# A graph network kernel on one core: the last large loop in another order, and its residual added by an accumulating transfer

## The chip, the cores and the metric

The kernel runs on one NeuronCore of a Trainium2 chip. The metric is the device time of one execution in microseconds (us), less is better. The engines are named as the profile names them: PE (TensorE) multiplies matrices, DVE (VectorE) works element by element and reduces, ACT (ScalarE) applies functions and copies, POOL (GpSimd) issues the transfers that need software, and SP (SyncE) issues the plain ones. Each engine runs its own list of instructions in order and waits on semaphores.

## The reference, cut to what matters

Four layers of a graph network run over 10,000 rows of 512 numbers, with 2,500 edges between them. After each layer the row is added to the layer's output and normalised. In float32 throughout:

```
x1 = LN(x + L0(x))                         # messages over the edges, then two dense products on all rows
p  = mean of neighbours @ W_l + b_l + x1 @ W_r
x2 = LN(x1 + leaky(batchnorm(p)) + x1)     # L1 adds its own input once more: 2 * x1 + leaky(...)
x3 = LN(x2 + L2(x2))                       # L2 and L3 are not zero only on rows that are the source of an edge
out = LN(x3 + L3(x3))                      # attention over the edges
```

`leaky(v)` is `max(v, 0.01 v)`, and the batch norm is one scale and one shift for each column. A row that is no source of an edge gets nothing from L2 and L3. For it the output is three layer norms in a row of `2 * x1 + leaky(scale * p + shift)`, which are folded into one with a changed epsilon. The kernel calls these the plain rows and computes them for all rows; the rows with edges are overwritten at the end.

## The kernel before

Rows are padded to 10,240, which makes 80 tiles of 128. The edges make 20 tiles of 128 (`EDGE_TILES`). Phases follow one another: messages, dense products over all tiles, aggregation, edge rows, then `values_phase`, which this change edits, and `attended_rows_phase`, which overwrites the rows with edges. Tables such as `p`, `x1`, `sum2` and `state` lie in memory (HBM).

`values_phase` is one software pipeline, unrolled in Python over `STEPS` = 25 steps. In step `s` tile `a = s` has its sums turned and multiplied, tile `b = s - 1` goes through the second product and a layer norm, tile `c = s - 2` gets queries and keys, tile `d = s - 3` scores, tile maxima and weighted values, and tile `e = s - 4` is merged into `state`. What a tile needs from another engine is reached by semaphores that count tiles.

For the maximum of a tile (`tile_maximum`, from L1762) the 8 scores of each of the 128 edges go to memory (`aw_rows`, issued by SP at L1458, 4 KB) and come back to all 128 partitions (`spread`, L1463, 512 KB). SP waits for the first transfer before it issues the second. The buffer `spread` lies in `same_dst`, which is its name in the profile, and `cand` lies in `filters`.

The plain rows are work without any tie to the edges, and fill idle time of DVE and ACT in the same loop. They are taken in 40 pairs of tiles (128 partitions, 2 rows of 512 each, 4 KB per partition). One pair is:

- SP: `pair_load` brings `p` and `x1`, 512 KB each (L1123, L1124), into one of two buffers each; the profile names the second `pair_x`.
- DVE: `pair_leaky` has three operations on 1,024 numbers per partition (L1138, L1140, L1142); `pair_moments` first forms `2 * x1 + leaky` (L1152) and then the statistics (L1156, L1159, L1161).
- ACT: `pair_normalise` has four small operations and two on a row each (L1171).
- SP: `pair_store` writes 512 KB (L1130).

How many pairs a step takes is in `HERE`, from `plain_plan`: 3, 2, 2, and from step 3 on 1 and 2 in turn. In a step with two pairs the first stands around `tile_maximum` on DVE and the second behind `softplus(a)`, which is the last thing on DVE that PE needs for its next step (`second(b, 0)` waits for it). ACT normalises the pairs of a step at the end of the same step, ahead of the copy (`second_product_out`) that empties PE's bank in the next.

Of the kernel before, what the change touches and what calls it, by code (L numbers as in the profile page):

```python
# [26 lines left out]
ALU = mybir.AluOpType  # L27
# [25 lines left out]
STATE = ATT + HEADS  # L53
LOG2 = 0.6931471805599453
# [1017 lines left out]
def tail_buffers(nc, k):  # L1072
# [5 lines left out]
    k.pair_p, k.pair_x1, k.pair_rows = (two(n, [P, 2, D]) for n in ("p", "x1", "rows"))  # L1078
# [4 lines left out]
    k.pair_p_in, k.pair_x1_in, k.pair_gone = (  # L1083
        [sem(f"{n}{i}") for i in range(2)] for n in ("p_in", "x1_in", "gone"))
    k.pair_scaled, k.pair_shifted, k.pair_leaky, k.pair_y, k.pair_st, k.pair_moments, k.pair_ready, k.pair_sc, k.pair_out = (
        sem(n) for n in ("scaled", "shifted", "leaky", "y", "st", "moments", "ready", "sc", "out"))


def norm_factors(norms):

    return (1.0, LN_EPS) if norms == 1 else (1.0 + LN_EPS + LN_EPS ** 2, LN_EPS ** 3)
# [20 lines left out]
def plain_plan(steps):  # L1112

    plan = [3, 2, 2] + [1 + i % 2 for i in range(steps - 3)]
    assert sum(plan) == PAIRS
    return plan


def pair_load(nc, k, sp, j):
    b, rows = j % 2, slice(j * 2 * P, (j + 1) * 2 * P)  # L1120
    if j >= 2:
        sp.wait_ge(k.pair_y, j - 1)
    sp.dma_start(k.pair_p[b][:, :, :], k.p[rows, :].rearrange("(p a) d -> p a d", a=2)).then_inc(k.pair_p_in[b], 16)  # L1123
    sp.dma_start(k.pair_x1[b][:, :, :], k.x1[rows, :].rearrange("(p a) d -> p a d", a=2)).then_inc(k.pair_x1_in[b], 16)  # L1124


def pair_store(nc, k, sp, j):
    b, rows = j % 2, slice(j * 2 * P, (j + 1) * 2 * P)
    sp.wait_ge(k.pair_out, 2 * (j + 1))
    sp.dma_start(k.out[rows, :].rearrange("(p a) d -> p a d", a=2), k.pair_rows[b][:, :, :]).then_inc(k.pair_gone[b], 16)  # L1130


def pair_leaky(nc, k, dve, j):
    b = j % 2
    a = k.pair_p[b][:, :, :]
    wide = lambda row: row[:, :].rearrange("p (a d) -> p a d", a=1).to_broadcast([P, 2, D])
    dve.wait_ge(k.pair_p_in[b], 16 * (j // 2 + 1))
# [7 lines left out]

def pair_moments(nc, k, dve, j):
    b = j % 2
    dve.wait_ge(k.pair_leaky, j + 1)
    dve.wait_ge(k.pair_x1_in[b], 16 * (j // 2 + 1))
    if j >= 2:  # L1150
        dve.wait_ge(k.pair_gone[b], 16 * (j // 2))
    nc.vector.scalar_tensor_tensor(out=k.pair_rows[b][:, :, :], in0=k.pair_x1[b][:, :, :], scalar=2.0,  # L1152
                                   in1=k.pair_p[b][:, :, :], op0=ALU.mult, op1=ALU.add).then_inc(k.pair_y, 1)
    dve.wait_ge(k.pair_y, j + 1)
    for s in range(2):
        nc.vector.bn_stats(k.pair_stats[b][:, s, :], k.pair_rows[b][:, s, :]).then_inc(k.pair_st, 1)  # L1156
    for s in range(2):
        dve.wait_ge(k.pair_st, 2 * j + s + 1)
        nc.vector.bn_aggr(k.pair_mv[b][:, s, :], k.pair_stats[b][:, s, :]).then_inc(k.pair_moments, 1)  # L1159
    dve.wait_ge(k.pair_moments, 2 * j + 2)  # L1160
    nc.vector.tensor_scalar(k.pair_neg[b][:, :], k.pair_mv[b][:, :, 0], -1.0, None, ALU.mult).then_inc(k.pair_ready, 1)  # L1161


def pair_normalise(nc, k, act, j):
# [3 lines left out]
                         k.pair_sc, 4 * j, norms=3)  # L1168
    for s in range(2):
        row = k.pair_rows[b][:, s, :]  # L1170
        nc.scalar.activation(row, row, ACT.Identity, bias=k.pair_shift[b][:, s:s + 1],  # L1171
                             scale=k.pair_rstd[b][:, s:s + 1]).then_inc(k.pair_out, 1)
# [211 lines left out]
def values_phase(nc, k):  # L1384
# [3 lines left out]
    with phase(nc, "f_") as (sb, ps, sem), ExitStack() as ctx:  # L1388
        T, AHEAD, STEPS = EDGE_TILES, 6, EDGE_TILES + 5
# [10 lines left out]
        spread, prod, q = slots(0, 8).rearrange("p (e h) -> p e h", h=HEADS), slots(8, KB), slots(12, KB)  # L1400
# [45 lines left out]
        def _(sp):  # L1446
            for out, w in ((w1s, k.L2_o1s), (w1v, k.L2_o1v), (w2s, k.L2_o2s), (w2v, k.L2_o2v)):
                sp.dma_start(out[:, :], w).then_inc(w_in, 16)
            pair_load(nc, k, sp, 0)
            pair_load(nc, k, sp, 1)  # L1450
# [3 lines left out]
            for step in range(STEPS):  # L1454
                t = step - 3
                if 0 <= t < T:
                    sp.wait_ge(aw_done, t + 1)
                    sp.dma_start(k.aw_rows[t, :].rearrange("(p h) -> p h", h=HEADS), k.scores[:, t, :]  # L1458
# [4 lines left out]
                    sp.dma_start(spread[:, :, :].rearrange("p e h -> p (e h)"),  # L1463
                                 k.aw_rows[t:t + 1, :].to_broadcast([P, P * HEADS])).then_inc(spread_in, 16)
                for _ in range(HERE[step - 1] if step else 0):
                    if pair + 2 < PAIRS:
                        pair_load(nc, k, sp, pair + 2)
                    pair_store(nc, k, sp, pair)
                    pair += 1
# [7 lines left out]
        def _(pool):  # L1477
# [20 lines left out]
            gather_state(0)  # L1498
            for step in range(STEPS):
# [120 lines left out]
        def _(act):  # L1620
# [76 lines left out]
            for step in range(STEPS):  # L1697
                a, b, c, d, e = step, step - 1, step - 2, step - 3, step - 4
                if 0 <= b < T:
                    second_product_out(b, 0)  # L1700
                if 0 <= c < T:
                    x3_turned_out(c, 0)
                    x3_turned_out(c, 1)
                if 0 <= b < T:
# [3 lines left out]
                if 0 <= e < T:  # L1708
                    state_factors(e)
                if 0 <= d < T:  # L1710
                    away_from(d)
# [12 lines left out]
                for _ in range(HERE[step]):  # L1724
# [342 lines left out]
```

## Time and profile before

| | |
|---|---|
| median of 3 runs | 2432.24 us (2429.86 to 2434.51) |
| the profiled execution: time / span | 2433.44 us / 2431.7 us |
| busy over the span | PE 78%, DVE 65%, ACT 43%, POOL 39% |
| `values_phase` | about 1731 to 2338 us, a quarter of the span |

A row of a timeline gives start, duration, engine, line, operation, result and operands, the number of instructions merged, and in brackets how long the engine sat idle before it and what it waited for. A line number is one of the kernel before. In this kernel the plain rows are spread over the whole of `values_phase`, so that the question for each wait is which engine ends it last.

### The profile page before, as it was taken

To read this page: it belongs to the slowest core of one execution; us is meant where nothing else is said; L and a number is where in the kernel's file an instruction comes from. 1 tells how busy PE (TensorE), PEld (TensorE's weight loads), DVE (VectorE), ACT (ScalarE), POOL (GpSimd) and SP (SyncE) were. 2 spreads that over 40 slices of the span, in tenths; PEclk is the share of its full clock that TensorE was granted. 3 is DMA by queue.
4 is the path that set the end of the run, shared out by engine and by line. 5 is a ranking of instruction groups with operands and counts; after the bars stand their busy time and mean duration, and the time that the engine had idled before them with its cause. 6 is when DMAs were issued, how large, how long until landed. Compare 5 with 4: busy or idle time off the path is not lost. (4 is left out here: it accounts for less than half of the span.)

```text
span 2431.7 us, 23979 instructions
## 1 busy us (share of the span) xinstructions
PE 1893.0 (78%) x5496; PEld 939.5 (39%) x5496; DVE 1588.0 (65%) x2664; ACT 1057.3 (43%) x2019; POOL 945.2 (39%) x1055
## 2 busy tenths in 40 slices
PE   5999995999999999999998492255378887888400
PEld 2444442444444444444444241133244444444200
DVE  5464551677777777777775051799467787777864
ACT  2343442455555555555554131244355544454222
POOL 2211111566666565666665633465211111111124
PEclk9999997999999999999999796555579998899755
DMA  7732124444444444444443734333533433434433
GB/s 263 246 117 56 18 26 90 144 145 157 153 151 159 143 165 143 161 148 156 154 148 112 212 44 75 94 87 78 192 131 123 160 131 130 176 129 148 165 123 109
DMA packets 152093, 326.07 MB, mean 134 GB/s; under 512 B 21969, under 2 KB 35186, under 8 KB 151766
## 3 DMA queue, kind: packets, MB, share of 16 engines
q1 hardware_dynamic: 120518, 244.22, 29.0%
q0 software_dynamic: 28160, 76.53, 12.7%
q10 hardware_dynamic: 3344, 4.51, 0.6%
q8 instruction: 28, 0.46, 0.1%
q14 instruction: 43, 0.35, 0.0%
HBM read 185.35 MB, written 139.84 MB: 134 GB/s over the span
## 5 line engine op out<-in xcount | busy, mean ns | idle before, releaser
L661 PE MATMUL d_p_h<-w3a,d_xT 128*128 128x512 f32 x640 | 290.5, 597 | 25.3 <-DMA d_xT<-in_xT 25.3
L661 PE MATMUL d_p_o<-d_w,d_uT 128*128 128x512 f32 x640 | 291.1, 598 | 3.0 <-ACT d_uT L736 3.0
L661 PE MATMUL d_p_p<-d_wr,d_x1T 128*128 128x512 f32 x640 | 290.4, 597 | 0.0
L818 DVE TENSOR_TENSOR d_zz<-d_yg,d_xbeta 128x512 f32<-128x512 f32 x80 | 138.5, 1732 | 98.8 <-POOL d_yg L869 98.8
L550 POOL TENSOR_SCALAR d_small<-d_mv 128x1 f32<-128x1 f32 x160 | 81.8, 512 | 306.3 <-DVE d_mv L787 156.4
L661 PEld LDWEIGHTS d_p_h<-w3a,d_xT 128*128 128x128 f32 x640 | 122.6, 192 | 180.8 <-issue 180.8
L661 PEld LDWEIGHTS d_p_o<-d_w,d_uT 128*128 128x128 f32 x640 | 122.3, 192 | 157.4 <-issue 152.8
L1482 POOL DMA_INDIRECT f_sums<-sum,index x40 | 44.4, 1110 | 323.3 <-PE f_p_T L1518 312.2
L729 ACT ACTIVATE d_yn<-d_y,d_small 128x512 f32<-128x512 f32 x80 | 65.1, 814 | 231.9 <-POOL d_small L555 231.9
L661 PEld LDWEIGHTS d_p_p<-d_wr,d_x1T 128*128 128x128 f32 x640 | 116.6, 192 | 116.9 <-issue 116.9
L282 PE MATMUL m_p_H<-m_xT,m_w 128*128 128x512 f32 x320 | 146.9, 613 | 4.8 <-ACT m_xT L323 4.8
L757 ACT ACTIVATE d_x<-d_zz,d_small 128x512 f32<-128x512 f32 x80 | 65.1, 813 | 178.5 <-POOL d_small L555 178.5
L499 DVE TENSOR_SCALAR m_h<-m_p_H,m_bias 128x512 f32<-128x512 f32 x40 | 30.0, 750 | 151.8 <-issue 98.5
L552 POOL TENSOR_TENSOR d_small<-d_small,minus_half 128x1 f32<-128x1 f32 x160 | 113.0, 706 | 13.3
L869 POOL TENSOR_TENSOR d_yg<-d_yn,d_gamma_row 128x512 f32<-128x512 f32 x80 | 115.9, 1448 | 0.0
L811 DVE TENSOR_SCALAR d_low<-d_h 128x512 f32<-128x512 f32 x80 | 111.7, 1396 | 2.7
L376 ACT ACTIVATE m_den<-m_low 128x512 f32<-128x512 f32 x40 | 25.2, 630 | 188.4 <-DVE m_low L504 188.3
L863 POOL TENSOR_TENSOR d_xb<-d_x,d_b_row 128x512 f32<-128x512 f32 x80 | 101.4, 1267 | 12.4 <-DMA d_x<-in_x 12.4
L211 POOL DMA_INDIRECT sum<-m_tile_sum,unique x20 | 31.2, 1559 | 191.3 <-ACT m_tile_sum L339 175.3
L850 POOL TENSOR_TENSOR d_xbeta<-d_x,d_beta_row 128x512 f32<-128x512 f32 x80 | 101.5, 1268 | 0.0
L780 DVE TENSOR_TENSOR d_y<-d_p_o,d_xb 128x512 f32<-128x512 f32 x80 | 55.3, 692 | 68.2 <-PE d_p_o L661 68.2
L200 POOL DMA_INDIRECT m_x_in<-in_x,index x40 | 44.4, 1110 | 135.3 <-PE m_p_T L238 121.9
(250 smaller groups left out, 4215.8 us busy)
## 6 DMA issues: line engine op xcount, KB each, us to landing
state<-d_empty SPq DMA_DIRECT2D x80, 264.0 KB, 2.1
sum<-m_tile_sum SPq DMA_DIRECT2D x10, 2048.0 KB
d_xT<-in_xT SPq DMA_DIRECT2D x80, 256.0 KB
d_z<-sum SPq DMA_DIRECT2D x80, 256.0 KB
d_x<-in_x SPq DMA_DIRECT2D x80, 256.0 KB
x<-d_x SPq DMA_DIRECT2D x80, 256.0 KB
p<-d_p SPq DMA_DIRECT2D x80, 256.0 KB
pair_p<-p SPq DMA_DIRECT2D x40, 512.0 KB
```

The source lines that it names most:

```text
L282: pe.matmul(out, w1[:, s * KB + b, cols], xT[:, g % 2, s, b, :], start=(s == 0 and b == 0), stop=False)
L550: nc.gpsimd.tensor_scalar(tmp, var, factor, add, ALU.mult, ALU.add).then_inc(done, 1)
L552: nc.gpsimd.tensor_tensor(rstd, tmp, k.minus_half[:, 0:1], ALU.pow).then_inc(done, 1)
L661: last = nc.tensor.matmul(out[:, :], lhsT[:, c, :], w[:, c, :], start=(c == 0), stop=(c == KB - 1))
L729: nc.scalar.activation(yn[b][:, :], y[b][:, :], ACT.Identity, bias=small[b][:, 0, 2:3], scale=small[b][:, 0, 1:2]).then_inc(yn_done, 1)
L757: nc.scalar.activation(x1[b][:, :], zz[b][:, :], ACT.Identity, bias=small[b][:, 1, 2:3], scale=small[b][:, 1, 1:2]).then_inc(x1_done, 1)
L780: nc.vector.tensor_tensor(y[b][:, :], p_o[b][:, :], xb[b][:, :], ALU.add).then_inc(y_done, 1)
L811: nc.vector.tensor_scalar(low[b][:, :], h[b][:, :], MISH_ONE, None, ALU.min).then_inc(low_done, 1)
L818: nc.vector.tensor_tensor(zz[b][:, :], yg[b][:, :], xbeta[b][:, :], ALU.add).then_inc(zz_done, 1)
L850: nc.gpsimd.tensor_tensor(xbeta[b][:, :], x[b][:, :], beta_row[:, :], ALU.add).then_inc(xbeta_done, 1)
L863: nc.gpsimd.tensor_tensor(xb[b][:, :], x[b][:, :], b4_row[:, :], ALU.add).then_inc(xb_done, 1)
L869: nc.gpsimd.tensor_tensor(yg[b][:, :], yn[b][:, :], gamma_row[:, :], ALU.mult).then_inc(yg_done, 1)
```

## The change

The diff does six things.

- The loop is one step shorter (`STEPS` = 24) and the pairs are planned as 3, 3, 2, 2, and then 2 and 1 in turn from step 4.
- `x1` is no longer loaded into its own buffer. After `pair_leaky` POOL issues a transfer that reads `x1` in memory and adds it onto the pair in place (`pair_residual`). Since a transfer can add but not double, the batch norm's scale and shift are halved once (`halve_norm`), and epsilon is divided by 4. L1152 is gone.
- `p` has four buffers (`PAIR_BUFS`). A load waits until ACT is done with the pair four earlier, and stands behind the store of that pair.
- On DVE `pair_moments` of a pair stands before `pair_leaky` of the following one. In a step with two pairs the sequence around `softplus(a)` is leaky, softplus, moments of the same pair, leaky of the next. `merge` moves between the two `moments`, and `tile_maximum` in front of all pairs.
- On ACT the pairs of a step are normalised in the next step, all but the last in its middle; `away_from`, `state_factors` and `weights` move forward.
- `spread` is laid out by head rather than by edge. `cand` is now read in order; in exchange the 4 KB write of the scores is scattered in memory, number by number.

```diff
+PAIR_BUFS = 4
...
-    return (1.0, LN_EPS) if norms == 1 else (1.0 + LN_EPS + LN_EPS ** 2, LN_EPS ** 3)
+    return (1.0, LN_EPS) if norms == 1 else (1.0 + LN_EPS + LN_EPS ** 2, LN_EPS ** 3 / 4)
...
-    plan = [3, 2, 2] + [1 + i % 2 for i in range(steps - 3)]
+    plan = [3, 3, 2, 2] + [2 - i % 2 for i in range(steps - 4)]
...
 def pair_load(nc, k, sp, j):
...
+    b = j % PAIR_BUFS
+    if j >= PAIR_BUFS:
+        sp.wait_ge(k.pair_out, 2 * (j - PAIR_BUFS + 1))
+    sp.dma_start(k.pair_p[b][:, :, :], pair_rows_of(k.p, j)).then_inc(k.pair_p_in[b], 16)
...
+def halve_norm(nc, k, dve):
+    for row in (k.bn_scale, k.bn_shift):
+        nc.vector.tensor_scalar(row[:, :], row[:, :], 0.5, None, ALU.mult).then_inc(k.halved, 1)
+    dve.wait_ge(k.halved, 2)
...
+def pair_residual(nc, k, pool, j):
+
+    b = j % PAIR_BUFS
+    pool.wait_ge(k.pair_leaky, j + 1)
+    nc.gpsimd.dma_start(k.pair_p[b][:, :, :], pair_rows_of(k.x1, j), accum_op=ALU.add).then_inc(k.pair_y[b], 16)
...
 def pair_moments(nc, k, dve, j):
...
-    nc.vector.scalar_tensor_tensor(out=k.pair_rows[b][:, :, :], in0=k.pair_x1[b][:, :, :], scalar=2.0,
-                                   in1=k.pair_p[b][:, :, :], op0=ALU.mult, op1=ALU.add).then_inc(k.pair_y, 1)
-    dve.wait_ge(k.pair_y, j + 1)
+    dve.wait_ge(k.pair_y[b], 16 * (j // PAIR_BUFS + 1))
...
-                    sp.dma_start(k.aw_rows[t, :].rearrange("(p h) -> p h", h=HEADS), k.scores[:, t, :]
+                    sp.dma_start(k.aw_rows[t, :].rearrange("(h p) -> p h", h=HEADS), k.scores[:, t, :]
...
+                if step:
+                    for j in range(pair, pair + HERE[step - 1]):
+                        pair_store(nc, k, sp, j)
+                        if j + PAIR_BUFS < PAIRS:
+                            pair_load(nc, k, sp, j + PAIR_BUFS)
+                    pair += HERE[step - 1]
...
+                for j in range(pair, pair + HERE[step]):
+                    pair_residual(nc, k, pool, j)
+                pair += HERE[step]
...
                 if 0 <= b < T:
                     moments(b, 0)
-                    moments(b, 1)
                 if 0 <= e < T:
                     merge(e)
...
+                if 0 <= b < T:
+                    moments(b, 1)
                 if 0 <= d < T:
                     tile_maximum(d)
...
+                if pair:
+                    pair_moments(nc, k, dve, pair - 1)
+                pair_leaky(nc, k, dve, pair)
                 if 0 <= d < T:
                     weigh_values(d)
                 if a < T:
                     softplus(a)
...
+                for j in range(pair + 1, pair + HERE[step]):
+                    pair_moments(nc, k, dve, j - 1)
+                    pair_leaky(nc, k, dve, j)
+                pair += HERE[step]
+            pair_moments(nc, k, dve, PAIRS - 1)
```

The order on DVE in step 4, a step with two pairs, from the end of the merge on. `pair_p0` and `pair_p1` are buffers of two pairs, `pair_x10` is buffer 0 of `pair_x1`, `filters` is `cand`, and `f_outT0<-f_logs,f_pos` is the end of `softplus`. Before:

```order
L1816 TENSOR_TENSOR f_new<-f_new,f_part 128x520
L1138 TENSOR_TENSOR pair_p0<-pair_p0,bn_scale 128x1024
...
L1142 SCALAR_TENSOR_TENSOR pair_p0<-pair_p0 128x1024
L1768 TENSOR_TENSOR filters<-same_dst,f_away 128x1024
L1774 TENSOR_REDUCE f_old1<-filters 128x8
...
L1152 SCALAR_TENSOR_TENSOR pair_rows0<-pair_x10,pair_p0 128x1024
L1156 BN_STATS pair_stats0<-pair_rows0 128x6 x2
...
L1785 TENSOR_TENSOR f_both<-f_p_qv,f_both 128x8x64
...
L1737 SCALAR_TENSOR_TENSOR f_outT0<-f_logs,f_pos 128x2x128
L1138 TENSOR_TENSOR pair_p1<-pair_p1,bn_scale 128x1024
...
L1156 BN_STATS pair_stats1<-pair_rows1 128x6 x2
...
L1757 TENSOR_TENSOR same_dst<-f_p_k,same_dst 128x512
```

The same place of the changed kernel, whose lines bear other numbers:

```order
L1841 TENSOR_TENSOR f_new<-f_new,f_part 128x520
L1768 BN_STATS f_stats1<-f_y1 128x6
...
L1793 TENSOR_TENSOR filters<-same_dst,f_away 128x1024
...
L1171 BN_STATS pair_stats1<-pair_p1 128x6 x2
...
L1150 TENSOR_TENSOR pair_p2<-pair_p2,bn_scale 128x1024
...
L1154 SCALAR_TENSOR_TENSOR pair_p2<-pair_p2 128x1024
L1810 TENSOR_TENSOR f_both<-f_p_qv,f_both 128x8x64
...
L1762 SCALAR_TENSOR_TENSOR f_outT0<-f_logs,f_pos 128x2x128
L1171 BN_STATS pair_stats0<-pair_p2 128x6 x2
...
L1150 TENSOR_TENSOR pair_p3<-pair_p3,bn_scale 128x1024
...
L1154 SCALAR_TENSOR_TENSOR pair_p3<-pair_p3 128x1024
L1782 TENSOR_TENSOR same_dst<-f_p_k,same_dst 128x512
```

The tile maximum has moved ahead of all pair work. The statistics of `pair_p2` stand two operations (`f_both` and `softplus`) behind its last leaky operation, and between these two now lies POOL's transfer.

SP's list from the scores of one tile to those of the next, with two pairs between them. Before:

```order
L1458 DMA aw_rows<-scores 128x8
L1463 DMA same_dst<-aw_rows 128x1024
L1123 DMA pair_p1<-p 128x1024
L1124 DMA pair_x11<-x1 128x1024
L1130 DMA out_rows<-pair_rows1 128x1024
L1123 DMA pair_p0<-p 128x1024
L1124 DMA pair_x10<-x1 128x1024
L1130 DMA out_rows<-pair_rows0 128x1024
L1458 DMA aw_rows<-scores 128x8
```

Changed, up to the next tile's `spread`:

```order
L1474 DMA aw_rows<-scores 128x8x1
L1479 DMA same_dst<-aw_rows 128x1024
L1136 DMA out_rows<-pair_rows0 128x1024
L1131 DMA pair_p2<-p 128x1024
L1136 DMA out_rows<-pair_rows1 128x1024
L1131 DMA pair_p3<-p 128x1024
L1474 DMA aw_rows<-scores 128x8x1
L1479 DMA same_dst<-aw_rows 128x1024
```

The loads of `x1` are gone from SP's list (40 in all), and a load now stands behind the store of the pair four earlier. POOL's list gains 40 transfers `pair_p<-x`, each behind `gather_state` of its step.

## Rows read from the trace of the kernel before

**Rows 1.** Busy time of the engines in three stretches of `values_phase`: head, loop, tail.

```profile
core 0: us, PE busy (x) PEld busy (x) DVE busy (x) ACT busy (x) POOL busy (x), PEclk, DMA share, GB/s
1731.00:1807.60 76.60, 41.44 (x130) 23.96 (x130) 51.61 (x81) 34.29 (x77) 13.82 (x13) 0.65 0.53 198
1807.60:2286.00 478.40, 385.81 (x1294) 205.39 (x1294) 367.00 (x582) 230.00 (x548) 77.23 (x64) 0.90 0.43 145
2286.00:2338.00 52.00, 8.12 (x16) 4.27 (x16) 42.10 (x62) 14.86 (x38) 4.38 (x3) 0.57 0.46 167
```

**Rows 2.** Timeline of SP: a one-pair step, a two-pair step, the last store.

```profile
2010.46 0.33 SPq L1458 DMA_DIRECT2D aw_rows<-scores  x1
2034.16 0.33 SPq L1458 DMA_DIRECT2D aw_rows<-scores  x1
2035.57 0.32 SPq L1463 DMA_DIRECT2D same_dst<-aw_rows  x1
2062.34 0.33 SPq L1458 DMA_DIRECT2D aw_rows<-scores  x1
...
2335.10 0.33 SPq L1130 DMA_DIRECT2D out_rows<-pair_rows  x1
```

**Rows 3.** Timeline of DVE in the two-pair step from 2034 to 2062 us.

```profile
2039.93 0.69 DVE L1743 BATCH_NORM_STATS2 f_stats<-f_y 128x6 f32<-128x512 f32 x1 [1.86 <-ACT f_y L1661]
...
2040.95 0.70 DVE L1806 TENSOR_TENSOR f_new<-f_old,f_factor 128x520 f32<-128x520 f32 x1
...
2042.98 1.22 DVE L1138 TENSOR_TENSOR pair_p<-pair_p,bn_scale 128x1024 f32<-128x1024 f32 x1
...
2046.64 2.00 DVE L1768 TENSOR_TENSOR filters<-same_dst,f_away 128x1024 f32<-128x1024 f32 x1
...
2050.04 1.23 DVE L1152 SCALAR_TENSOR_TENSOR pair_rows<-pair_x,pair_p 128x1024 f32<-128x1024 f32 x1
...
2052.95 0.69 DVE L1785 TENSOR_TENSOR f_both<-f_p_qv,f_both 128x512 f32<-128x512 f32 x1
...
2054.22 1.22 DVE L1138 TENSOR_TENSOR pair_p<-pair_p,bn_scale 128x1024 f32<-128x1024 f32 x1
...
2057.99 1.22 DVE L1152 SCALAR_TENSOR_TENSOR pair_rows<-pair_x,pair_p 128x1024 f32<-128x1024 f32 x1
2059.25 1.29 DVE L1156 BATCH_NORM_STATS2 pair_stats<-pair_rows 128x6 f32<-128x512 f32 x2
...
2060.89 0.69 DVE L1757 TENSOR_TENSOR same_dst<-f_p_k,same_dst 128x512 f32<-128x512 f32 x1
```

**Rows 4.** Timeline of ACT: the copy that frees PE's bank, behind that step's last pair.

```profile
2063.49 0.57 ACT L1661 ACTIVATE f_y<-f_p_R 128x512 f32<-128x512 f32 x1
```

**Rows 5.** DMA issues of the whole kernel: result and operands, count, median us to landing.

```profile
sum<-m_tile_sum,unique POOLq DMA_INDIRECT x20, 4.8
...
sum<-e_tile_sum,unique POOLq DMA_INDIRECT x20, 3.8
...
aw_rows<-scores SPq DMA_DIRECT2D x20, 4.0 KB, 1.4
state<-f_new,unique POOLq DMA_INDIRECT x20, 3.0
```

**Rows 6.** Timeline of POOL: an accumulating write of 256 KB, a plain one of 264.

```profile
1404.85 1.79 POOL L926 DMA_INDIRECT p<-dst_rows_sb,unique  x1 [3.97 <-DMA p<-dst_rows_sb,unique]
...
2046.59 1.00 POOL L1493 DMA_INDIRECT state<-f_new,unique  x1 [0.31 <-issue]
```

**Rows 7.** DMA from 1859.0 to 1876.0 us, 40 slices: SP's queue after a tile's scores.

```profile
GB/s 10 0 0 48 270 289 212 222 193 231 241 222 260 299 434 386 366 434 443 414 395 443 405 414 424 434 415 405 424 174 48 0 96 193 19 248 388 0 0 0
```

**Rows 8.** DMA queue share from 2034.0 to 2036.0 us, which is one write of `aw_rows`.

```profile
q1 hardware_dynamic: 144, 0.00, 3.8%
```

**Rows 9.** Timeline of DVE: the last tile's scores and its maximum.

```profile
2286.68 0.69 DVE L1759 TENSOR_REDUCE scores<-same_dst 128x8 f32<-128x512 f32 x1
...
2293.99 1.98 DVE L1768 TENSOR_TENSOR filters<-same_dst,f_away 128x1024 f32<-128x1024 f32 x1
```

More of the change, by code:

```diff
@@ L1077, in tail_buffers @@
     two = lambda name, shape: [sb(f"{name}{i}", shape) for i in range(2)]
-    k.pair_p, k.pair_x1, k.pair_rows = (two(n, [P, 2, D]) for n in ("p", "x1", "rows"))
+    k.pair_p, k.pair_rows = [sb(f"p{i}", [P, 2, D]) for i in range(PAIR_BUFS)], two("rows", [P, 2, D])
     k.pair_stats, k.pair_mv = two("stats", [P, 2, 6]), two("mv", [P, 2, 2])
@@ L1082, in tail_buffers @@
     k.eps_set = sem("eps_set")
[L1083 to L1086, printed above, removed]
+    k.pair_p_in, k.pair_y, k.pair_gone = (
+        [sem(f"{n}{i}") for i in range(count)] for n, count in (("p_in", PAIR_BUFS), ("y", PAIR_BUFS), ("gone", 2)))
+    k.halved = sem("halved")
+    k.pair_scaled, k.pair_shifted, k.pair_leaky, k.pair_st, k.pair_moments, k.pair_ready, k.pair_sc, k.pair_out = (
+        sem(n) for n in ("scaled", "shifted", "leaky", "st", "moments", "ready", "sc", "out"))
 def norm_factors(norms):
-    return (1.0, LN_EPS) if norms == 1 else (1.0 + LN_EPS + LN_EPS ** 2, LN_EPS ** 3)
+    return (1.0, LN_EPS) if norms == 1 else (1.0 + LN_EPS + LN_EPS ** 2, LN_EPS ** 3 / 4)
 def set_eps(nc, k, pool):
@@ L1168, in pair_normalise @@
                          k.pair_sc, 4 * j, norms=3)
+    if j >= 2:
+        act.wait_ge(k.pair_gone[b], 16 * (j // 2))
     for s in range(2):
-        row = k.pair_rows[b][:, s, :]
-        nc.scalar.activation(row, row, ACT.Identity, bias=k.pair_shift[b][:, s:s + 1],
+        nc.scalar.activation(k.pair_rows[b][:, s, :], k.pair_p[j % PAIR_BUFS][:, s, :], ACT.Identity, bias=k.pair_shift[b][:, s:s + 1],
                              scale=k.pair_rstd[b][:, s:s + 1]).then_inc(k.pair_out, 1)
@@ L1448, in _ @@
                 sp.dma_start(out[:, :], w).then_inc(w_in, 16)
[L1449 to L1450 removed]
+            for j in range(PAIR_BUFS):
+                pair_load(nc, k, sp, j)
             sp.dma_start(k.wqk, k.L3_W[:, 0:2 * D].rearrange("(c p) n -> p c n", p=P)).then_inc(k.wqk_in, 16)
@@ L1462, in _ @@
                         sp.wait_ge(cand_done, t)
-                    sp.dma_start(spread[:, :, :].rearrange("p e h -> p (e h)"),
+                    sp.dma_start(spread[:, :, :].rearrange("p h e -> p (h e)"),
                                  k.aw_rows[t:t + 1, :].to_broadcast([P, P * HEADS])).then_inc(spread_in, 16)
[L1465 to L1469, printed above, removed]
+                if step:
[4 more added lines that the diff above has]
+                    pair += HERE[step - 1]
             while pair < PAIRS:
@@ L1498, in _ @@
             gather_state(0)
+            pair = 0
             for step in range(STEPS):
@@ L1696, in _ @@
             pair = 0
-            for step in range(STEPS):
+            for step in range(STEPS + 1):
                 a, b, c, d, e = step, step - 1, step - 2, step - 3, step - 4
+                late = HERE[step - 1] if step else 0
+                if 0 <= d < T:
+                    away_from(d)
                 if 0 <= b < T:
@@ L1707, in _ @@
                     sums_turned_out(a, 0)
[L1708 to L1711, printed above, removed]
+                for _ in range(late - 1):
+                    pair_normalise(nc, k, act, pair)
+                    pair += 1
                 if 0 <= c < T:
@@ L1723, in _ @@
                     logarithms(a)
-                for _ in range(HERE[step]):
+                if late:
                     pair_normalise(nc, k, act, pair)
@@ L1847, in _ @@
                     softplus(a)
-                for _ in range(extra - 1):
-                    pair_leaky(nc, k, dve, pair)
-                    pair_moments(nc, k, dve, pair)
-                    pair += 1
+                for j in range(pair + 1, pair + HERE[step]):
[3 more added lines that the diff above has]
+            pair_moments(nc, k, dve, PAIRS - 1)
 def attended_rows_phase(nc, k):
```

48 lines of the change are left out of this document (18 added, 30 removed).

## Prediction

> **What bounds the kernel now.** I first read the busy time by stretches [rows 1], since the change touches only `values_phase`. In its loop (1807.6 to 2286 us, 19 steps) PE is busy 385.8 of 478.4 us and DVE 367.0. Neither is full, so the steps have to be looked at singly. SP's writes of the scores mark them [rows 2]: a step with one pair takes 2034.16 - 2010.46 = 23.7 us, one with two pairs 2062.34 - 2034.16 = 28.2.
>
> DVE's timeline shows why [rows 3]. In the two-pair step the second pair stands behind `softplus(a)`, from 2054.22 to 2060.89. ACT normalises it only then, in order, and the copy that frees PE's bank comes at 2063.49 [rows 4]. In the next steps PE starts late and DVE waits for `f_y`, as in the row at 2039.93 (1.86 us idle). So the loop now runs round PE, ACT and DVE in turn, with no wait for a transfer: `cand` starts right behind DVE's own work at 2046.64, 12.5 us after the scores went out, and even behind the last tile, where only 7.3 us lie between the start of the last scores operation and `cand` (2286.68, 2293.99), it has no wait [rows 9].
>
> **What DVE has to do afterwards.** From the starts in [rows 3]: the three leaky operations take 2057.99 - 2054.22 = 3.77 us, the sum with `x1` 2059.25 - 2057.99 = 1.26, the statistics 2060.89 - 2059.25 = 1.64, `merge` 2042.98 - 2040.95 = 2.03, the tile maximum 2050.04 - 2046.64 = 3.40, weighting and `softplus` 2054.22 - 2052.95 = 1.27. The scores take 1.4 (2060.89 to the write at 2062.34, [rows 2, 3]). The change takes away 1.26 for each of 40 pairs, 50 us, and `cand`, read in order, should fall from 2.00 to the 1.22 of its neighbours of the same size, 16 us over 20 tiles; the maximum becomes 2.6. `halve_norm` adds two operations of 512 columns, some 1.2 us together by half of the 1.22 for 1,024 each; they lie in the wait for the first pair and cost nothing (1.2 if that wait were gone). ACT's late pair no longer stands in front of the copy. Were nothing late, the loop would approach PE's 385.8 us, and the gain would be tens of microseconds.
>
> **What becomes late: the residual.** Each pair now goes leaky (DVE), transfer (POOL), moments (DVE). In a two-pair step only weighting and `softplus`, 1.27 us, lie between leaky and moments of the first pair, and between pairs of a three-pair step nothing. DVE waits in order, and behind it stand the next leaky and then the next tile's scores, for which SP, ACT and PE wait. So the price is the time from the end of leaky to landing, W. The trace has no such transfer of 512 KB into SBUF. The accumulating write of 256 KB (`m_tile_sum`, 128x512) lands 4.8 us after its issue, that of 128 KB (`e_tile_sum`, 128x256) 3.8 [rows 5]. That is 1.0 us per 128 KB, so 4.8 + 2.0 = 6.8 for 512 KB, an estimate. In a chain of such writes POOL issues for 1.79 us and then sits idle for 3.97 until landing [rows 6], 5.8 in all, so the way back to a waiting engine can add up to 1. Bounds: a plain scatter of 264 KB lands in 3.0 [rows 5]; the other half of 512 KB at 400 GB/s [rows 7] adds 0.65 and the longer issue 1.79 - 1.00 = 0.8 [rows 6], so 4.5 from below. From above 6.8 plus half of the 1 MB of store and load that may run beside it (1.3 at 400 GB/s), 8.1. I take W = 6.8, the value of the rows of its own kind.
>
> The Trainium skill ("Collectives: The Full Stack", section "The bandwidth ceiling: the fold count and why AG ≠ RS ≠ AR") says that an add in a DMA costs no time of its own but reads two sources, which halves the rate. By that rule W would be 4.5 and 1.3 for the second read, 5.8, and the sum below 20 us less, 2429, which is rival (2). The trace does not side with it for writes to memory: 128 KB per us is a third of the 400 GB/s of plain transfers, not a half.
>
> **What becomes late: `spread`.** `tile_maximum` moved forward, to 1.4 + 0.4 + 2.03 = 3.8 us after the start of the scores in a one-pair step, and to about 7 in a two-pair step, where `moments(b, 1)` waits for PE and ACT. The write lands in 1.4 [rows 5]. `spread` is issued then; the queue moves about 240 GB/s at first [rows 7], so 512 KB take 2.2, and with start and landing I put 3.6. That is 1.4 + 1.4 + 3.6 = 6.4 after the start of the scores, and it was hidden before. Now three things come on top. The write is in single numbers (8 x 128, and 16 for the semaphore): 144 packets took 3.8% of 16 engines over 2 us, 8.4 ns each [rows 8], so 1,040 add 0.5. After a two-pair step the residual of the second pair runs beside it: up to its 4 us of transfer, I take 2.4. After a one-pair step SP issues a store and a load, 1 MB and 2.6 us [rows 7], in front of the write in the same queue, and is itself some 0.5 late: 3.1. So `spread` is there at 9.3 in a one-pair and 10.0 in a two-pair step. Bounds: 1 to 2.4 less where the queues interleave well; 1 more where they don't.
>
> Of the scattered write the skill ("DMA: Bandwidth & Descriptors", "Rules for kernel authors") says that a last dimension that is not contiguous becomes one descriptor for each element; no row here shows what one of 4 bytes costs, and the 0.5 stands on the size of those of 32 bytes.
>
> **The sum, against the profiled execution.** Head: DVE takes its first pair near 1737 and reaches the first scores at 1807.6, 70.6 us. Afterwards 8 leaky and 7 moments stand there, with a bare wait before each moments: 8 x 3.77 + 7 x 1.64 + 6 x 6.8 + 9 = 91.5. The 9 is the first wait, beside 3 MB of weights in the same DMA engines. That is +21.
>
> Loop: a one-pair step is 9.3 + 2.6 + 1.64 + 3.77 + 1.27 = 18.6 (shorter than PE's 385.8 / 19 = 20.3, which can run over into the longer neighbour). A two-pair step is 10.0 + 2.6 + 1.64 + 3.77 + 6.8 + 1.64 + 3.77 = 30.2. From step 3 to 21 there are 10 of two and 9 of one: 302 + 167 = 469, against 478.4: -9.
>
> Tail: before, 2286.7 to the last store at 2335.1 is 48.4 [rows 2, 9]. Afterwards 30.2, then 6.8 + 1.64 + 3.77 for the last pair, 6.8 + 1.64 for its moments, and 2.6 for ACT, 53.5: +5.
>
> In all +17, from 2433.4 to 2450; the median of the runs, 2432.2, is 1.2 lower: **2449 us**. About 20 waits carry W, so each microsecond of it moves the sum by 20, and so does each of `spread`. It breaks even at W = 6.0.
>
> **Rivals.** (1) The residual lands cheaply. For it: the destination is SBUF, so the read of the old value needs no second trip to memory, and rows are 4 KB instead of 2. Against it: both sizes in [rows 5] lie on a steep line. With W = 5.2 and `spread` 1 us earlier the sum is 17 - 32 - 20 = -35, 2398. It decides from W = 6.0 down. (2) The adding itself is free and only the second read of 512 KB counts: W = 4.5 + 1.3 = 5.8, the sum -3, 2429; the gain of the new order is spent on the waits, and the result lies within 5 us of before. For it: nothing in the rows says that reads from SBUF are as slow as those from memory. Against it: the steep line again. This is where the skill's rule ends. (3) The engines of the DMA fill up. They are 43% busy in the loop [rows 1]; three residuals of 4 us in 49 add 25 points, and they fall into the same moments as `spread`, store and load. With W = 8.1 and `spread` 1 later: 17 + 26 + 20 = +63, 2495. Against it: the mean leaves room.
>
> **How the numbers follow.** Two medians of this kernel can be told apart by about 0.2%, 5 us. I give 0.47 to my forecast (its own range 2438 to 2478), 0.08 to (3), 0.15 to (2), 0.30 to (1). From these, slower 0.55, same 0.15, faster 0.30. Leaving one in ten at either end gives 2400 to 2480.
>
> **What would show it.** Right: DVE rows of `pair_stats` with some 5 us idle before them that end at the transfer `pair_p<-x`, 20 times; landing of that transfer near 6.8; the first scores near 1828; `cand` at 1.2 and with idle time that ends at a DMA in most steps; two-pair steps near 30, one-pair steps near 19. Wrong: a landing under 6 and two-pair steps under 28; or one-pair steps above 20 in which DVE waits for PE or ACT, which would mean that I drew the loop too short.

## The result and the profile after

The changed kernel takes 2651.92 us (median of 4 runs, 2650.84 to 2655.52), the kernel before beside it 2433.38 (4 runs). The ratio is 1.0901, 95% interval 1.0882 to 1.0920: 9% slower. The direction was forecast, the size was not: +17 us forecast, about +219 measured.

The same three stretches as in [rows 1]. The inner borders lie about 1 us behind the start of the first and of the last scores operation (1837.6 and 2496.3):

```profile
core 0: us, PE busy (x) PEld busy (x) DVE busy (x) ACT busy (x) POOL busy (x), PEclk, DMA share, GB/s
1731.00:1838.70 107.70, 48.55 (x160) 27.79 (x160) 47.82 (x81) 41.06 (x90) 20.40 (x21) 0.65 0.57 161
1838.70:2497.40 658.70, 416.11 (x1266) 220.61 (x1267) 319.39 (x561) 225.10 (x545) 93.06 (x94) 0.78 0.51 106
2497.40:2560.00 62.60, 7.48 (x15) 3.49 (x14) 25.40 (x44) 10.52 (x27) 6.52 (x7) 0.55 0.44 96
```

Head +31.1, loop +180.3, tail +10.6. In the loop DVE has 47.6 us less to do and yet the loop is longer. PE has the same matmuls (5,496 in the kernel before and in this one), but in the loop its busy share fell from 81% to 63%, the granted clock from 0.90 to 0.78, and its busy time grew by 30 us. The page's groups for DVE, ACT and PE name what they idle for (last columns: idle time before them, and what ended it):

```profile
L1793 DVE TENSOR_TENSOR filters<-same_dst,f_away 128x1024 f32<-128x1024 f32 x20 | 24.5, 1225 | 264.2 <-DMA same_dst<-aw_rows 264.2
L1171 DVE BATCH_NORM_STATS2 pair_stats<-pair_p 128x6 f32<-128x512 f32 x80 | 51.3, 684 | 113.8 <-DMA pair_p<-x 113.8
L1708 ACT ACTIVATE f_both<-f_less 128x8 f32<-128x8 f32 x20 | 4.3, 215 | 280.7 <-DVE f_less L1803 280.7
L1608 PE MATMUL f_p_S<-f_both,same_src 128*128 128x260 f32 x80 | 42.0, 681 | 229.4 <-DVE f_both L1810 229.4
```

In the kernel before, the same two groups of ACT and PE:

```profile
L1687 ACT ACTIVATE f_both<-f_less 128x8 f32<-128x8 f32 x20 | 4.3, 216 | 85.4 <-DVE f_less L1778 85.4
L1587 PE MATMUL f_p_S<-f_both,same_src 128*128 128x260 f32 x80 | 25.8, 449 | 30.4 <-DVE f_both L1785 30.2
```

DVE has two waits for transfers that it did not have before: 114 us for the residual (20 times), and 264 us for the broadcast of the scores (20 times). ACT idles 195 us more and PE 199 more in front of what `cand` leads to (`f_less`, `f_both`): that is the second wait passed on. The landing times (from issue until the data is there) say why (compare [rows 5], where the write of `aw_rows` lands after 1.4 us and the scatter of `state` after 3.0):

```profile
pair_p<-x POOLq DMA_DIRECT2D x40, 512.0 KB, 5.6
...
same_dst<-aw_rows SPq DMA_DIRECT2D x20, 512.0 KB, 4.9
...
aw_rows<-scores SPq DMA_DIRECT2D x20, 4.0 KB, 13.5
...
state<-f_new,unique POOLq DMA_INDIRECT x20, 8.3
```

A write of 4 KB now lands after 13.5 us. SP's timeline, a one-pair step from write to write and the broadcast behind it (compare [rows 2]):

```profile
2124.23 0.37 SPq L1474 DMA_DIRECT2D aw_rows<-scores  x1
2137.37 0.32 SPq L1479 DMA_DIRECT2D same_dst<-aw_rows  x1
...
2153.22 1.69 SPq L1474 DMA_DIRECT2D aw_rows<-scores  x1
2167.94 0.32 SPq L1479 DMA_DIRECT2D same_dst<-aw_rows  x1
```

The broadcast is issued 13.1 us behind the write; before it was 1.4. A one-pair step now takes 2153.22 - 2124.23 = 29.0 us, the two-pair step behind it, to the next write at 2193.54, 40.3 (23.7 and 28.2 before). DVE meanwhile:

```profile
2122.80 0.68 DVE L1782 TENSOR_TENSOR same_dst<-f_p_k,same_dst 128x512 f32<-128x512 f32 x1
...
2142.21 1.23 DVE L1793 TENSOR_TENSOR filters<-same_dst,f_away 128x1024 f32<-128x1024 f32 x1 [13.87 <-DMA same_dst<-aw_rows]
```

19.4 us from the start of the scores to `cand` in this one-pair step, where 9.3 were forecast. And yet the queue looks idle. DMA queues of 2124.2 to 2137.5 us, while the write is under way (packets, MB, share of 16 engines):

```profile
q0 software_dynamic: 320, 1.06, 68.7%
q1 hardware_dynamic: 1040, 0.00, 4.5%
```

1,040 packets, 4.5% of 16 engines over 13.3 us: 9.2 ns each, about the price that the prediction took from [rows 8]. The packets are as cheap as forecast; their landing is not.

### The profile page after: what moved, and what is told of

Its sections match the earlier page's. It is cut to its first block and busy times, and to the rows that moved or that the text cites. A ratio compares the mean times of both kernels' runs of the same rounds, so it can differ in the third digit from the quotient of the medians.

```text
span 2653.8 us, 23978 instructions
## 1 busy us (share of the span) xinstructions
PE 1923.8 (72%) x5496; PEld 957.1 (36%) x5496; DVE 1519.9 (57%) x2626; ACT 1054.0 (40%) x2019; POOL 969.7 (37%) x1095
## 3 DMA queue, kind: packets, MB, share of 16 engines
q1 hardware_dynamic: 132678, 223.24, 25.2%
## 5 line engine op out<-in xcount | busy, mean ns | idle before, releaser
L1608 PE MATMUL f_p_S<-f_both,same_src 128*128 128x260 f32 x80 | 42.0, 681 | 229.4 <-DVE f_both L1810 229.4
L1162 POOL DMA_DIRECT2D pair_p<-x x40 | 38.1, 952 | 426.1 <-DVE pair_p L1154 414.2
L1793 DVE TENSOR_TENSOR filters<-same_dst,f_away 128x1024 f32<-128x1024 f32 x20 | 24.5, 1225 | 264.2 <-DMA same_dst<-aw_rows 264.2
L553 POOL TENSOR_TENSOR d_small<-d_small,minus_half 128x1 f32<-128x1 f32 x160 | 113.0, 706 | 13.3
L1171 DVE BATCH_NORM_STATS2 pair_stats<-pair_p 128x6 f32<-128x512 f32 x80 | 51.3, 684 | 113.8 <-DMA pair_p<-x 113.8
L1608 PEld LDWEIGHTS f_p_S<-f_both,same_src 128*128 128x128 f32 x80 | 23.5, 324 | 249.8 <-DVE f_both L1810 246.0
L1579 PE MATMUL f_p_qv<-wv,column_acc 128*128 128x512 f32 x160 | 96.8, 761 | 18.4 <-ACT same_dst L1696 18.3
```

What stands on the lines that cost most here:

```text
L553: nc.gpsimd.tensor_tensor(rstd, tmp, k.minus_half[:, 0:1], ALU.pow).then_inc(done, 1)
L1171: nc.vector.bn_stats(k.pair_stats[c][:, s, :], k.pair_p[b][:, s, :]).then_inc(k.pair_st, 1)
L1579: last = nc.tensor.matmul(out[:, :], xT[:, c, :], w[:, c, :], start=(c == 0), stop=(c == KB - 1))
L1608: last = nc.tensor.matmul(p_S[:, half, 0:ATT // 2].rearrange("p (h f) -> p h f", h=HEADS // 2), k.same_src[:, t, :], both[:, hs, :], start ...
```

## The experiments

The theory of the loss, A: the write in 4-byte pieces side by side lands late, whatever else runs, and each tile waits for it; the residual's wait comes on top. Its rivals: the new order or the adding transfer does most of it.

**One part undone, one part alone.** `e1_by_edge` is the changed kernel with the scores' table as before:

```
-    sp.dma_start(k.aw_rows[t, :].rearrange("(h p) -> p h", h=HEADS), k.scores[:, t, :]
+    sp.dma_start(k.aw_rows[t, :].rearrange("(p h) -> p h", h=HEADS), k.scores[:, t, :]
```

(with `spread` and `cand` to match). `e2_before_by_head` is the kernel before with the opposite edit and nothing else.

> The changed kernel with one part undone: the scores go to memory in pieces of 8 numbers as before, spread is laid out by edge and cand reads it with a stride. Theory A, the write in single numbers is what costs (landing 13.5 us instead of 1.4): the write lands in under 4 us, the 264 us that DVE waits for spread fall to under 80, cand goes back to 2.0 us, and the time is 2425 to 2455, which is what the prediction had for the rest of the change. Theory B, the write is late because stores, loads and the adding transfers stand before or beside it: it still lands after 8 us or more and the time stays above 2550.

> The kernel before with only this part done: the scores are written in single numbers and cand reads in order. Theory A: the write lands in 12 to 14 us, spread arrives some 18 us after the scores, cand needs it after 12, so about 20 waits of 5 to 7 us less 16 us for the faster cand: 2510 to 2560. Theory B: no adding transfers here and the write is ahead of the loads in its queue, so it lands in under 4 us and the time is 2415 to 2435.

By edge: 2488.77 us, 1.0235 of before (1.0218 to 1.0252). By head in the old order: 2564.07, 1.0536 (1.0519 to 1.0554). So the layout alone costs 132 us in the old order and 163 in the new. That is A, though its numbers were missed on both sides: by head the write held SP for 11.2 us and not 12 to 14, and the time is 4 us above my range. DVE's waits in `e2_before_by_head` are not where I put them either:

```profile
L1138 DVE TENSOR_TENSOR pair_p<-pair_p,bn_scale 128x1024 f32<-128x1024 f32 x40 | 48.8, 1220 | 102.1 <-DMA pair_p<-p 102.1
L1768 DVE TENSOR_TENSOR filters<-same_dst,f_away 128x1024 f32<-128x1024 f32 x20 | 24.5, 1225 | 50.2 <-DMA same_dst<-aw_rows 50.2
```

`cand` waits only ten times, in every second step. Two thirds of the waiting is for `p`: SP stands waiting for the landing of the scores, and the loads of the next pairs stand behind it in SP's list. With two buffers for `p` that reaches DVE; in the changed kernel, with four and another order, the same group waits for 2.5 us.

By edge the changed kernel is still 56 us slower than before, where I had expected -7 to +23. The write landed after 4.8 us (under 4 expected), and DVE waited 88.1 us in front of `cand` (under 80 expected). Its landings and SP's timeline:

```profile
aw_rows<-scores SPq DMA_DIRECT2D x20, 4.0 KB, 4.8
```

```profile
2054.30 0.32 SPq L1474 DMA_DIRECT2D aw_rows<-scores  x1
2059.47 0.32 SPq L1479 DMA_DIRECT2D same_dst<-aw_rows  x1
```

Even in 32-byte pieces the write lands after 4.8 us there and not after 1.4.

**The transfer alone.** `e3_dve_residual` is the by-edge kernel in which DVE adds the residual from a loaded copy; to make room the pairs have three buffers and the gathers run four ahead. `e9_by_head_dve` is the same by head.

```
-                for j in range(pair, pair + HERE[step]):
-                    pair_residual(nc, k, pool, j)
+    nc.vector.scalar_tensor_tensor(out=k.pair_p[b][:, :, :], in0=k.pair_x1[c][:, :, :], scalar=2.0,
+                                   in1=k.pair_p[b][:, :, :], op0=ALU.mult, op1=ALU.add).then_inc(k.pair_sum, 1)
```

> e1_by_edge with the residual taken back to DVE: x1 is loaded by SP into two buffers, p has three, the gathers run 4 instead of 6 ahead so that it fits; order of the loop and plan as in the change. Theory A': the waits for the adding transfer (114 us in 20 waits) are the price of the transfer, so DVE's 50 us of additions replace them and the time falls by 40 to 65 below e1_by_edge, to about 2385. Rival: they lie beside waits for PE and ACT, and the time is that of e1_by_edge within 10 us.

> The changed kernel, scores side by side by head as it has them, but the residual by VectorE from a loaded copy: the scattered write without the adding transfer. Beside it stand the same kernel by edge (2372 us) and the changed one (2652 us). If the two costs add, it is 2372 + 163 = 2535 us; theory A of the loss (each tile's scores wait for a write that lands after 12 us or more whatever else runs): 2510 to 2560. Rival (the write is only slow because the adding transfer is beside it): under 2440.

`e3_dve_residual`: 2372.34 us, 0.9764 of before (0.9744 to 0.9784), with nothing left out. That is 116 us below the by-edge kernel, where my theory said 40 to 65: it had left out that the wait in front of `cand` would shrink too. The 113.6 us of waits for the transfer are gone, that one fell from 88.1 to 39.7, and DVE has 47 us more to do: 113.6 + 48.4 - 47 = 115. `e9_by_head_dve`: 2532.61, 1.0424 (1.0402 to 1.0446).

In the new order the costs add up: the adding transfer costs 116 us by edge and 119 by head, the layout 163 with it and 160 without. The new order by itself, with that kernel's buffers and gathers, is worth -61; what these two side changes do is not separated. Without the adding transfer the median landing of the by-edge write is 2.0 us, and of the one by head 10.7.

**What of the transfer costs.** `e6_plain_pool`: by edge, without `accum_op`, so the plain rows' own part is left out. `e8_small_add`: by edge, adding, but 64 of 1,024 values a row pair; the rest of the residual is left out.

```
-    nc.gpsimd.dma_start(k.pair_p[b][:, :, :], pair_rows_of(k.x1, j), accum_op=ALU.add)
+    nc.gpsimd.dma_start(k.pair_p[b][:, :, :], pair_rows_of(k.x1, j))                               (e6)
+    nc.gpsimd.dma_start(k.pair_p[b][:, 0:1, 0:64], pair_rows_of(k.x1, j)[:, 0:1, 0:64], accum_op=ALU.add)  (e8)
```

> The kernel with scores by edge, whose transfer on POOL's queue writes x1 over the rows instead of adding to them (the plain rows' own part is left out). Theory A (the engines that add read both operands, and that is what makes 512 KB land after 5.5 us): it lands after 3 to 3.5 us, 20 waits shrink by 2 to 2.5 us each, the time falls by 40 to 60 us to 2430 to 2450. Theory B (the landing is what a transfer of 512 KB on this queue takes beside the others): it lands after 5 us or more, and the time stays within 2475 to 2490.

> The kernel with scores by edge, whose adding transfer carries 64 of a row pair's 1,024 values (32 KB instead of 512 KB; the rest of the residual is left out). Theory A (its bytes hold up the write and the broadcast of the scores): the scores' write lands after 2 us or less instead of 4.8, the wait for the transfer falls by half, and the time is 2370 to 2410, as with the residual on VectorE. Theory B (the new order alone makes the write late, by the stores and loads beside it): the write still lands after 4 us or more, and the time is 2430 or more.

`e6_plain_pool`: 2422.86 us; the transfer lands after 3.8 us instead of 5.5, the waits for it fall from 113.6 to 80.4 us, and the scores' write lands after 3.1. `e8_small_add`: 2371.58; its 32 KB land after 2.6 us, the scores' write after 2.0, and the waits on `pair_stats` are 51.1 us, 19 of them. Both theories A hold in the main: adding costs 1.7 us over writing, and the bytes of this transfer hold up the scores. The plain landing was slower than the 3 to 3.5 us that I expected and the gain (66 us) larger than 40 to 60, since two waits shrank: the one in front of `cand` fell too, from 88.1 to 62.8.

The medians of the scores' write hide two groups, though. The distance from the write to the broadcast in SP's timeline, from the fourth to the nineteenth tile:

| us | behind a two-pair step | behind a one-pair step |
|---|---|---|
| adding, 512 KB (`e1_by_edge`) | 4.5 to 5.2 | 5.4 to 6.1 |
| plain, 512 KB (`e6_plain_pool`) | 2.8 to 3.3 | 4.8 to 5.9 |
| adding, 32 KB (`e8_small_add`) | 1.6 to 2.4 | 3.9 to 4.6 |
| none (`e3_dve_residual`) | 1.4 to 1.8 | 4.6 to 5.1 |

Behind a one-pair step SP has issued a store and one or two loads right in front of the write. So the adding transfer holds up one half of the writes, and what SP itself put in front of them holds up most of the other half.

**The wait for the residual covered.** `e5_late_moments` is the by-edge kernel, `e10_head_late` the changed one, each with this edit:

```
-                    pair_moments(nc, k, dve, j - 1)
                     pair_leaky(nc, k, dve, j)
+                    pair_moments(nc, k, dve, j - 1)
```

> The kernel with scores by edge, and in a step with two or three pairs the moments of a pair behind the leaky of the next, so that 3.77 us of VectorE's own work lie between a pair's leaky and the moments that wait for the adding transfer; nothing is left out. Theory A (the adding transfer's 5.5 us landing is exposed because nothing of VectorE's lies behind the leaky, and VectorE sets the step): 16 pairs gain up to 3.77 us each, at most 60 us; the wait for pair_p<-x falls from 113.6 us to 40 to 60 and the time from 2488.8 to 2430 to 2460. Theory B (the chain of a tile's scores through memory sets the step, and VectorE waits there if it doesn't wait here): the wait moves to the filters line, and the time stays within 2475 to 2490.

> The changed kernel with the moments of a pair behind the next leaky, as in the by-edge kernel that went from 2489 to 2391 us; nothing is left out. Theory A (with the write landing after 12 us or more, the chain of the scores through memory sets the step, and VectorE's wait for the adding transfer is inside it): it gains under 40 us, time over 2612, and the wait for the broadcast stays over 230 us. Rival (both waits are in line): it gains 80 to 110 us, 2540 to 2570.

`e5_late_moments`: 2390.75 us, 0.9826 of before (0.9806 to 0.9845), with nothing left out: 98 us less than the by-edge kernel for two lines exchanged. `e10_head_late`: 2540.08, 112 less than the changed kernel; there my theory was wrong, and the rival right. DVE takes its work in order, so its two waits in a step add up; the second does not swallow the first. From the by-edge kernel to `e5_late_moments`:

```profile
L1171 DVE BATCH_NORM_STATS2 pair_stats<-pair_p 128x6 f32<-128x512 f32 x80 | 51.3, 684 | 113.6 <-DMA pair_p<-x 113.6
```

```profile
L1171 DVE BATCH_NORM_STATS2 pair_stats<-pair_p 128x6 f32<-128x512 f32 x80 | 51.3, 683 | 40.9 <-DMA pair_p<-x 40.9
```

73 us less there, and 26 less (88.1 to 61.9) in front of `cand`: 99 of 98. My bound of 60 was wrong twice. It counted only the first of these, and in that only the 16 exchanged places; but a wait at the start of the next step shrinks as well, since the moments that moved stand in front of it (in the head seven waits of 48.6 us in all became five of 19.6). In `e10_head_late` it was 114 to 41, and 264 to 222.

**Is it the number of pieces or where they lie?** `e7_apart` is the changed kernel with each score written 512 bytes from the next, as many pieces of 4 bytes; the broadcast reads other rows of 4 KB, so the scores of other edges are left out of the maximum.

```
-    sp.dma_start(k.aw_rows[t, :].rearrange("(h p) -> p h", h=HEADS), k.scores[:, t, :]
+    sp.dma_start(k.aw_rows[t, :].rearrange("(h p g) -> p h g", h=HEADS, g=128)[:, :, 0:1],
+                 k.scores[:, t, :].rearrange("p (a b) -> p a b", b=1)
```

> The changed kernel with the 1,024 scores of a tile written 512 bytes apart instead of side by side, still 4 bytes a packet and as many packets; the broadcast reads 4 KB of the plain rows in their place (the scores of other edges are left out of the maximum). In the probe such a write landed after 2.6 and 2.8 us, the side-by-side one after 8.6 and 11.5 us. Theory N (4-byte writes are slow where their neighbours in memory are written by other engines at the same moment): the write lands after 4 to 6 us, and the time falls from 2652 to 2440 to 2500. Theory C (1,024 packets are slow whatever their addresses, once other traffic is beside them): it lands after 10 us or more and the time stays over 2600.

2497.09 us, 1.0255 (1.0236 to 1.0275), at 132,678 packets on q1 as in the changed kernel. That is within 9 us of the by-edge kernel: the 4-byte pieces cost little once they do not lie side by side. The landing is 1.1 us above the by-edge one, some 22 us over 20 tiles, and the shorter `cand` takes 16 of that back:

```profile
aw_rows<-scores SPq DMA_DIRECT2D x20, 4.0 KB, 5.9
```

**The write by itself.** `e4_probe` and `e11_probe_spacing` are the kernel before with small transfers ahead of the loop, each waited for before the next, each form twice:

```
+    for name, out, a in forms:
+        for _ in range(2):
+            sp.dma_start(out, a).then_inc(done, 16)
+            n += 1
+            sp.wait_ge(done, 16 * n)
```

> The kernel before with seven small transfers put ahead of the loop, two of each, every one awaited and nothing else under way: 4 KB to memory in pieces of 32 bytes; of 8; of 4; 2 KB in pieces of 4; 4 KB in pieces of 4 that lie 512 bytes apart; 4 KB read from memory in pieces of 4; 4 KB within SBUF in pieces of 4. If the number of pieces sets the time (some 12 ns each): 1.4, 7, 13, 7, 13, 13, 13 us. If it is neighbouring pieces in memory that hold each other up: the pieces 512 bytes apart, the read and the one within SBUF land in under 5. If it is only the crowd in the loop: all under 4.

> The kernel before, and ahead of its loop small writes to memory one after another, each waited for, each twice: 1,024 pieces of 4 bytes side by side, and 8, 16, 32, 64 and 128 bytes apart; 512 pieces 8 bytes apart, the four of a 32-byte block from one partition; 128 pieces side by side. Side by side 1,024 landed after 8.6 and 11.5 us before, 512 bytes apart after 2.6 and 2.8 us. Theory N (writers of neighbouring addresses wait for each other): the landing falls with the distance, to under 3 us at 64 or 128 bytes, and 512 pieces whose block is written from one partition land faster than the 10.8 us of 512 side by side. Theory C (it is the number of pieces, and the wide case was fast for another reason): all of 1,024 pieces land after 8 us or more, and 128 pieces after 1.5 to 2.5 us.

`e4_probe`, one profiled execution. DMA issues, each taken from its own narrow window (us to landing last): 4 KB in 4-byte pieces side by side, then 2 KB of them, then 4 KB of them 512 bytes apart:

```profile
probe_rows<-src_rows_sb SPq DMA_DIRECT2D x1, 4.0 KB, 11.5
...
probe_rows<-src_rows_sb SPq DMA_DIRECT2D x1, 2.0 KB, 10.8
...
probe_rows<-src_rows_sb SPq DMA_DIRECT2D x1, 4.0 KB, 2.6
```

The second write of each form took 11.5, 10.9 and 2.8 us against 8.6, 10.8 and 2.6 for the first. The remaining forms: in 32-byte pieces 1.4; in 8-byte pieces side by side 4.2 and 5.5; memory to SBUF in 4-byte pieces 2.1, SBUF to SBUF 2.3 (there 8 bytes apart, and each partition writes to itself). So of the forms tried only writes to memory are slow.

`e11_probe_spacing`, one profiled execution. SP's timeline; a write starts when the one before has landed, so the distance of two starts is a landing (`--dma` has 11.9, 4.3 and 3.1 for three of them). Two writes of each form in turn: 1,024 pieces of 4 bytes side by side, 8, 16, 32, 64 and 128 bytes apart, then 512 pieces 8 bytes apart, the four of a 32-byte block from one partition, then 128 pieces side by side:

```profile
1722.56 0.38 SPq L1400 DMA_DIRECT2D probe_rows<-src_rows_sb  x1
1731.98 0.37 SPq L1400 DMA_DIRECT2D probe_rows<-src_rows_sb  x1
1743.87 0.36 SPq L1400 DMA_DIRECT2D probe_rows<-src_rows_sb  x1
1748.19 0.36 SPq L1400 DMA_DIRECT2D probe_rows<-src_rows_sb  x1
1752.54 0.36 SPq L1400 DMA_DIRECT2D probe_rows<-src_rows_sb  x1
1755.67 0.36 SPq L1400 DMA_DIRECT2D probe_rows<-src_rows_sb  x1
1758.79 0.36 SPq L1400 DMA_DIRECT2D probe_rows<-src_rows_sb  x1
1761.38 0.36 SPq L1400 DMA_DIRECT2D probe_rows<-src_rows_sb  x1
1764.01 0.36 SPq L1400 DMA_DIRECT2D probe_rows<-src_rows_sb  x1
1766.36 0.36 SPq L1400 DMA_DIRECT2D probe_rows<-src_rows_sb  x1
1769.11 0.36 SPq L1400 DMA_DIRECT2D probe_rows<-src_rows_sb  x1
1771.80 0.36 SPq L1400 DMA_DIRECT2D probe_rows<-src_rows_sb  x1
1775.12 0.62 SPq L1400 DMA_DIRECT2D probe_rows<-src_rows_sb  x1
1778.50 0.54 SPq L1400 DMA_DIRECT2D probe_rows<-src_rows_sb  x1
1782.55 0.33 SPq L1400 DMA_DIRECT2D probe_rows<-src_rows_sb  x1
1789.64 0.34 SPq L1400 DMA_DIRECT2D probe_rows<-src_rows_sb  x1
```

From start to next start: 9.4 and 11.9 side by side, 4.3 twice at 8 bytes, 3.1 twice at 16, 2.6 twice at 32, 2.4 and 2.8 at 64, 2.7 and 3.3 at 128. The 512 pieces take 3.4 and 4.0; but 128 pieces side by side, an eighth of the number, take 7.1, and 8.6 the second time. So the nearness sets most of it and the number little (theory N). What fits all of them is how many packets go into one small stretch of memory, since 512 pieces of 8 bytes side by side (4.2, 5.5) cost about what 4-byte pieces 8 bytes apart do. Each form was written twice in one execution, so tenths should not be read into it. Why the memory or the engines are slow there stays open, and so does whether it matters which partitions write.

## Why the prediction was wrong

**What bounds the kernel, and what is removed:** right. `cand` fell to 1.22 us, and with the transfer's waits out of the way (`e3_dve_residual`) the new order gains 61 us, "tens of microseconds".

**The residual:** right in place and number, and right in size partly by luck. There are 20 waits. From the end of leaky to the moments, which is the W of the forecast, DVE's timeline has 5.7 to 6.3 us in nine of the ten loop places and 9.1 in the tenth, 5.7 in the tail, and 7.3 to 10.1 in the head: on average 6.9, where 6.8 was taken. The transfer alone lands after 5.6 us in the median, so the step from [rows 5] put it too high, and the slow waits of the head made up for it. The nine in the loop lie at the break-even of 6.0 and near the 5.8 of rival (2); neither (1) nor (2) came in the result, since `spread` outweighed both. The step of 1.0 us for each 128 KB, taken over from the writes to memory, was too steep: 32 KB land after 2.6 and 512 after 5.5, which is 0.77. The lower bound stood on a plain transfer, which lands after 3.8 us where 4.5 had been added up.

The Trainium skill ("Collectives: The Full Stack", "The bandwidth ceiling: the fold count and why AG ≠ RS ≠ AR") says that an add reads a second source. From the plain landing that is 3.8 + 1.3 = 5.1, an estimate with the 1.3 us of the prediction for 512 KB; measured 5.5, so the rule is nearer than my line from [rows 5].

**`spread`: the step that failed.** "1,040 add 0.5" prices the scattered write by the busy time of its packets. That busy time was right (9.2 ns a packet) and said nothing of the landing: 13.5 us in the changed kernel against 1.4 before, so 12.1 more where 0.5 was added. `cand` came 19.4 us after the start of the scores in the one-pair step and 21.3 (2151.33 to 2172.67) in the two-pair step, where 9.3 and 10.0 were forecast. In the by-edge kernel they are 11.9 (2052.87 to 2064.75) and 11.1 (2021.62 to 2032.76). Over all 20 tiles the means are 20.1 and 11.1: the layout makes `cand` late by 181 us in all, less 16 for its shorter run, 165 where 163 were measured. The Trainium skill ("DMA: Bandwidth & Descriptors", "Rules for kernel authors") warned of one descriptor for each element. The 1,040 packets are that, 1,024 and 16 more; but the warning has no time, and where the elements are written far apart they are cheap all the same (`e7_apart`). The prediction also had no rival for this term: its bounds ("1 more") came from other transfers in the queue, none from the write itself, and that is why the range missed.

**A smaller one in the same term.** By edge, `cand` still came 1.4 us later than forecast on average (11.1 against 9.7): the transfers beside and in front of it delay not only the broadcast but the 4 KB write as well (4.8 us), which the prediction left at 1.4. That is 28 us over 20 tiles; the steps there take 21.3 us with one pair and 31.1 with two, forecast 18.6 and 30.2. `cand`, which this layout leaves at 2.0 us, is another 16, and the head another 8 (first scores at 1835.7 instead of 1828). These 52 stand against the 39 between +17 and +56; W below 6.8 in loop and tail gives some 9 back.

**Head and tail.** Head of the changed kernel: first scores at 1837.6, forecast 1828. The seven waits cost what was forecast, 49.3 us in all against 6 x 6.8 + 9; the first pair began 2 us later, and some 7 us of the edges' own DVE work stood between the pairs, which the sum had left out. Tail: three waits of 3.1 to 5.7, and 15.6 for the last broadcast, where the forecast had `spread` at 10.0 and `cand` came at 20.0.

**Rival (3)** did not come: the DMA share is 0.51 in the loop (0.43 before), with GB/s down from 145 to 106. What grew was the time of one small write, not the load on the engines.

**The direction:** slower, as forecast, but 163 of the 219 us come from the term that had been put at 0.5 us a tile. Without it the changed kernel is still 56 us slower (`e1_by_edge`), which is what the +17 can be held against.

## What to carry to other kernels

A small transfer on a dependent chain is priced by its landing, never by bytes or packets' busy time; if the change gives it a form that no row shows, its upper bound is open, and the forecast has to say so. Do not write neighbouring 4-byte elements to memory from many partitions: keep a partition's elements together (32 bytes here) and let the reading engine take the stride, 0.78 us a tile here against some 9. Ask also what else stands behind a wait in the list of the issuing engine: in the old order most of the price was paid by loads behind it. Behind an operation that hands a buffer to a DMA, put other work of the same engine: the exchange of two lines was worth 98 us, and by edge, with it or with the addition back on VectorE, the new order beats the old by 1.7% and 2.4%.

## What the runs showed of the hardware

- 4 KB written to memory in 4-byte pieces side by side land after 8.6 to 11.9 us alone (`e4_probe`, `e11_probe_spacing`) and 13.5 in the loop of the changed kernel, against 1.4 in 32-byte pieces. The queue's share stays at 4.5%: the profile does not count this time as busy.
- The effect grows with nearness, and little with number: 128 pieces side by side 7.1 and 8.6 us, 1,024 pieces 8 bytes apart 4.3, 64 apart 2.4 and 2.8, 512 apart 2.6 and 2.8.
- The scatter of `state` lands later with it: 3.0 us before and 7.8 in the old order with the layout alone; 8.3 in the changed kernel and 3.1 with the pieces 512 bytes apart. Whether the write itself holds it up or the transfers that move beside it is not separated.
- An adding transfer of 512 KB from memory into SBUF lands after 5.5 us, a plain one after 3.8; POOL issues it in 0.95 us instead of 0.58. 32 KB adding take 2.6 to land.
- A 4 KB write that lands after 1.4 us by itself takes 4.5 to 5.2 beside that adding transfer (`e1_by_edge`), and 4.6 to 5.1 behind a store and two loads of 512 KB each in its own queue (`e3_dve_residual`).
